# Expert stage of a GNN layer with a mixture of experts: the parts of the chunk sorts and the chunk sizes moved in the plan

## The reference

```python
x = x + gnn(layernorm(x), edges)      # two segment sums over the edges, two 256x256 products, tanh
x = x + ffn(layernorm(x))             # below

rh = relu(f @ router_w1 + router_b1)                       # 256 -> 128
expert_logits = softmax(rh @ router_w2 + router_b2)        # 6 experts
top_w, top_i = top_k(expert_logits, 2)
routing_weights = softmax(top_w)
h1 = relu(f @ expert_w1[e] + expert_b1[e])                 # 256 -> 256, for every expert e
h2 = relu(h1 @ expert_w2[e] + expert_b2[e])
expert_out = h2 @ expert_w3[e] + expert_b3[e]
combined = sum over the two chosen experts of expert_out * routing weight
```

## Time and profile before

| | |
|---|---|
| time, median of 3 runs | 3660.32 us (3653.39 to 3662.05) |
| profiled execution: time, span | 3686.31 us, 3684.6 us |
| TensorE busy in the span | 2478.4 us, 67% |
| VectorE busy | 2074.6 us, 56% |
| ScalarE busy | 942.4 us, 26% |
| POOL busy | 2218.0 us, 60% |
| mean granted TensorE clock | 0.788 |
| last stage, first to last tile's addition | 3173.06 to 3660.97 us |

### The profile page before, as it was taken

The page is one execution under the profiler, slowest core; times in us unless marked ns, Lnnn a source line. Parts: engine busy times, 40 slices in busy tenths (PEclk is TensorE's granted clock), DMA queues, the critical chain, the costliest instruction groups (busy, mean ns, idle before and its releaser), DMA issues.

```text
span 3684.6 us, 37872 instructions
## 1 busy us (share of the span) xinstructions
PE 2478.4 (67%) x8589; PEld 1420.2 (39%) x8589; DVE 2074.6 (56%) x5241; ACT 942.4 (26%) x2586; POOL 2218.0 (60%) x2267
## 2 busy tenths in 40 slices
PE   6463355556655666658677777777777776689786
PEld 4343233334333333436223222222222322678675
DVE  8999444444444444445466656666666666545554
ACT  5686000000000000003222222222222224446342
POOL 5387566666666666666666666666666661225345
PEclk7667577777777677668788888888888887889887
DMA  0200433333333333344533333333333336225344
GB/s 23 71 3 10 140 90 93 93 89 93 90 94 89 92 92 91 92 88 77 158 91 91 91 90 92 92 90 90 92 90 93 92 87 122 88 70 164 92 119 125
DMA packets 169722, 334.22 MB, mean 91 GB/s; under 512 B 39463, under 2 KB 104704, under 8 KB 169508
## 3 DMA queue, kind: packets, MB, share of 16 engines
q0 software_dynamic: 100064, 264.05, 26.6%
q1 hardware_dynamic: 69444, 67.75, 5.6%
HBM read 289.39 MB, written 42.06 MB: 90 GB/s over the span
## 4 chain that ended last, share of the span: by engine, by line
PE 47%; DVE 20%; issue 13%; another core or an unknown queue 12%; DVEq 4%; ACT 3%; DMA 1%; POOL 0%; POOLq 0%; SPq 0%; ACTq 0%
PE ps L934 34%; DVE big L970 10%; PE ps L1693 5%; DVEq L943 3%; PE ps L1673 2%; DVE graph L963 2%; ACT big L574 2%; PE ps L1060 1%; DVE big L753 1%; DVE arena L745 1%; DVEq L970 1%; PE ps L1651 1%; PE ps L989 1%; DVE node L686 0%
## 5 line engine op out<-in xcount | busy, mean ns | idle before, releaser
L934 PE MATMUL ps<-arena,graph 128*128 128x258 f32 (+1 forms) x3588 | 1665.4, 608 | 876.6 <-DVE graph L963 528.4
L970 DVE TENSOR_TENSOR big<-ps,big 128x258 f32 (+1 forms) x1794 | 1003.3, 559 | 956.9 <-remote 420.0
L934 PEld LDWEIGHTS ps<-arena,graph 128*128 128x128 f32 x3588 | 758.8, 234 | 1775.5 <-issue 1674.2
L899 POOL DMA_INDIRECT arena<-xn_table,graph x897 | 849.3, 947 | 472.7 <-issue 202.4
L899 POOL DMA_INDIRECT arena<-h_table,graph x897 | 858.6, 957 | 447.7 <-issue 235.0
L963 DVE TENSOR_SCALAR graph<-iota,graph 128x128 f32<-128x128 f32 x1794 | 545.1, 304 | 310.2 <-issue 215.1
L915 ACT ACTIVATE arena<-arena 128x256 f32<-128x256 f32 x897 | 352.3, 413 | 951.0 <-PE ps L934 561.6
L1312 POOL DMA_INDIRECT arena<-xn_table,node x118 | 125.1, 1060 | 341.3 <-PE ps L1651 164.5
L998 ACT ACTIVATE late<-ps 128x256 f32<-128x256 f32 x49 | 18.8, 383 | 1150.1 <-remote 846.4
L493 POOL DMA_INDIRECT edge_list<-big x112 | 158.9, 1419 | 78.7 <-issue 78.7
L537 PE MATMUL ps<-big,arena 128*128 128x224 f16 x832 | 129.9, 327 | 104.1 <-ACT big L574 97.8
(11 more groups left out here) (252 smaller groups left out, 1823.0 us busy)
## 6 DMA issues: line engine op xcount, KB each, us to landing
y_table<-big SPq DMA_DIRECT2D x118, 128.0 KB
arena<-xn_table,graph POOLq DMA_INDIRECT x897
arena<-h_table,graph POOLq DMA_INDIRECT x897
xn_table<-node SPq DMA_DIRECT2D x7, 896.0 KB, 8.3
h_table<-node SPq DMA_DIRECT2D x7, 896.0 KB, 4.1
node<-in_x SPq DMA_DIRECT2D x1, 6144.0 KB
late<-h_table SPq DMA_DIRECT2D x12, 512.0 KB
big<-in_x SPq DMA_DIRECT2D x12, 512.0 KB, 4.6
```

What stands on the lines that cost most here:

```text
L899: e.indirect_dma_start(out=row, out_offset=None, in_=table, in_offset=bass.IndirectOffsetOnAxis(ap=idx[:, k:k + 1], axis=0)).then_inc(s_ro ...
L934: e.matmul(out_, hot[:, k % HOTS, :], moving, start=True, stop=True).then_inc(s_sum[i], 1)
L970: e.tensor_tensor(block, ps[a % BANKS][:, 0:width], block, ALU.add).then_inc(s_add[i], 1)
```

## The change

Three things change, all in the plan. The chunks become 16, 12, 12 and 9 blocks (16, 16, 12 and 5 before), with 37, 29, 29 and 23 tiles, again 118. TensorE's parts of a sort get names of their own: "sums" and "places" (`pe_sums`, `pe_places`; before, `pe_sort` was called for each step and acted in steps 3, 9 and 11). In the sorts of chunks 1 to 3 they stand one tick behind VectorE's step that feeds them, and VectorE's steps stand one to a tick (steps 1 and 2 share one, and step 12 stands with the last placing), so that a sort lasts 14 ticks instead of 7. The sort of chunk 0, ahead of the tiles, has them in the tick of the step as before. And a chunk's routes no longer begin at a chunk's first tile: they follow behind the routes of the chunk before, beside its sort.

```diff
-        cut = [0, 4, 8, 11, NG]
+        cut = [0, 4, 7, 10, NG]
...
-        SORT_STEPS = 13
+        SORT = ((0,), (1,), (2,), (3, "sums"), (4,), (5,), (6,), (7,), (8,), (9, "places"), (10,), (11, "places"), (12,))
+        SORT_SLOWLY = ((0,), (1, 2), (3,), ("sums",), (4,), (5,), (6,), (7,), (8,), (9,), ("places",), (10,), (11,),
+                       ("places", 12))
...
-            def sort_of(s, t, each):
-                for step in range(SORT_STEPS):
-                    put(t + step // each, "sort", s, step)
-                return t + -(-SORT_STEPS // each)
+            def sort_of(s, t, ticks_of):
+                halves = iter(range(2))
+                for i, steps in enumerate(ticks_of):
+                    for step in steps:
+                        if step == "sums":
+                            put(t + i, "sums", s)
+                        elif step == "places":
+                            put(t + i, "places", s, next(halves))
+                        else:
+                            put(t + i, "sort", s, step)
+                return t + len(ticks_of)
...
-            lead = sort_of(0, t, 1)
+            lead = t = z = sort_of(0, t, SORT)
             for s in range(1, NS):
-                t = z = lead + tile0[s - 1]
                 for i, pair in enumerate(pairs[s]):
                     if (s, i) != (1, 0):
                         t = x1_slowly(pair, t)
-                    z = route_slowly(pair, t)
+                    y = route_slowly(pair, t)
                     t += 2 + len(pair)
-                z = sort_of(s, z, 2)
+                t = y
+                z = sort_of(s, max(y, z), SORT_SLOWLY)
```

More of the change, by code:

```diff
@@ L1643, in pe_last @@
                     pe_route(e, n, step[0])
-                elif stage == "sort":
-                    pe_sort(e, n, step[0])
+                elif stage == "sums":
+                    pe_sums(e, n)
+                elif stage == "places":
+                    pe_places(e, n, step[0])
                 elif stage == "turn":
@@ L1726, in pe_route, with pe_sums, pe_places @@
                 m.then_inc(s_lg, 1)
-        def pe_sort(e, s, step):
+        def pe_sums(e, s):
+            n = len(chunks[s])
+            e.wait_ge(s_som, s + 1)
+            if s:
+                e.wait_ge(s_srt, s)
+            e.matmul(ps[7][:, 0:NE * n], below[:, :], member[:, 0:NE * n], start=True, stop=True)
+            e.matmul(ps[7][:, 256:256 + NE * n], ones[:, :], member[:, 0:NE * n], start=True,
+                     stop=True).then_inc(s_sob, 1)
+        def pe_places(e, s, c):
             n, nt = len(chunks[s]), tiles_in[s]
             th = tile_hot[:, 0:2 * n * nt].rearrange("p (a b j) -> p a b j", a=2, b=n)
[L1731 to L1744, removed]
+            e.wait_ge(s_lhot, 2 * s + c + 1)
+            for i in range(n):
+                m = e.matmul(ps[7][:, 0:2 * nt].rearrange("p (a j) -> p a j", a=2), lane_hot[:, i, :],
+                             th[:, :, i, :], start=(c == 0 and i == 0), stop=(c == 1 and i == n - 1))
+            m.then_inc(s_tokp, 1)
         block = ctx.enter_context(nc.Block())
```

## The result

| | before | after |
|---|---|---|
| time, median (us) | 3656.86 (3652.95 to 3662.05, 4 runs) | 3616.38 (3610.67 to 3621.89, 4 runs) |
| ratio to before | 1 | 0.9885, 95% interval 0.9871 to 0.9899 |
| profiled execution: time, span (us) | 3686.3, 3684.6 | 3621.9, 3620.2 |
| its ticks 1 to 117 (us) | 487.9 | 436.4 |
| behind the last tile (us) | 23.6 | 32.2 |

The change takes 40.5 us away; 39.4 had been forecast, from a median of 3660.3 to 3621 us. The two profiled executions differ by 64.4 us, and not all of that is the change's: tick 0 begins at 3151.59 instead of 3173.06, 21.5 us earlier, behind gathering passes that the change doesn't touch. The rest is 51.5 us less in the ticks (forecast 49.5) and 8.6 more behind them (forecast 10.1), 42.9 net.

The account below looks back on a forecast made before the run. TensorE bounds bare ticks at 2.87 us, VectorE's steps the sorts, POOL's gathers the end. Excess falls from 152.3 to 102.8 us, 49.5 less; the end adds 10.1: 39.4 off 3660.3 gives 3621 us, range 3596 to 3648.

Parts of the forecast that it names:

- Sorts bound by waits for each other: Sorts of chunks 1 to 3: VectorE's steps bound them, TensorE and VectorE waiting in turn; 72.5 of 152.3 us excess.
- Ticks 18 to 35: Sort of chunk 1 beside variations, x1 and routes: 22 us of excess (8 to 33), 12.1 of it VectorE's overhang.
- Ticks 43 to 60: Sort of chunk 2 with chunk 0's blocks brought back beside it: 28 us of excess (17 to 42), 7.5 for those blocks.
- Ticks 66 to 79: Sort of nine blocks with only blocks brought back beside it: about 5 us of excess (2 to 12).
- Ticks 1 to 17, 36 to 42: Stretches without sorts, carrying three groups and one group of side work: 11.1 and 3.7 us of excess.
- Blocks brought back: Excess where blocks return beside tiles, priced by rates from the trace: 31.5 us after the change (10 to 45).
- The end: After the last tile, nine blocks gathered instead of five: 8 x 1.27 = +10.1 us, uncertain by at most 1 us.
- Chunk borders and ScalarE's tables: First gathers of a chunk cost nothing; table load before the exponentials 1.5 us a sort, two further table changes at most 1.35 each.
- Overlap better than costed (3596): Rival 1, crowded stages: light ticks make up for heavy ones, excess only 8 and 17 us, 25 us more gone; chance 13%.
- Waits that only spread (3646): Rival 2: steps, exponentials, variations and stores wait for each other; crowded stages cost half as much again, 25 us; chance 12%.
- Half clock in the crowded stages (3680): Rival 3: TensorE at half rate through 36 crowded ticks, 1.65 us more each, 59 us less 39, slower; chance 6%.
- over 0.95: Sign that the forecast is right: TensorE's granted clock in ticks 18 to 60 lies above this value.

Follow-up runs that it names:

- behind only: Kernel before with its chunk sizes, only TensorE's sums and placings one tick behind VectorE's step: 3273.78 us, 0.9897 (second kind); again 3617.06, 0.9891 (first kind).

## Why the prediction was right, point by point

- *Sorts bound by waits for each other.* Right, and shown in both directions: put into the kernel before, the tick between the engines takes 41.8 us of the sorts' 71.1; taken out of the changed kernel, it gives 27.6 back. In the changed kernel TensorE waits 0.0 us before sums and placings.
- *Ticks 18 to 35.* Forecast 22 (74 us), measured 22.3 (73.9) and, on the second kind of chip, 21.6. Counting VectorE's overhang tick by tick gave the right sum; no run prices its terms one by one.
- *Ticks 43 to 60.* Forecast 28 (80 us), measured 32.1 (83.8) and 26.6 (78.3). One tick of 6.7 us is the longest of the run; under 7, as said. The 7.5 us in it were VectorE's additions for blocks brought back. No run takes them out: without POOL's gathers, but with the additions, the stage is 1.3 us shorter. But this stage is 5.0 us longer than that of ticks 18 to 35 on the second kind (78.27 less 73.24), where the forecast has 7.5 less 1.7 = 5.8 for the difference, so the size of the term fits.
- *Ticks 66 to 79.* Forecast 5; measured 8.0 and 3.7.
- *Ticks 1 to 17, 36 to 42.* Forecast 11.1 and 3.7; measured 10.4 and 3.7 (10.4 and 3.5).
- *Blocks brought back.* This is the step that failed, though the sum hid it. Since its ticks overlap those of the third sort, I compare ticks 61 to 117 as a whole: forecast 5 + 1.5 + 31.5 = 38.0; the first kind took 32.3 and the second 2.9. I had rates from one trace, read them as the price of a block at a given spacing, and expected thinner ones to cost less: 17.9 us less in all (8.9 + 25.7 + 14.8 = 49.4 before, 31.5 after). On the second kind eleven ticks with blocks as dense as any cost 0.6 us over bare ones. What the first kind takes longer in the stage hardly follows the spacing: 41.5 us in the kernel before (487.9 less 446.4), 39.8 in "behind only" (445.9 less 406.1), 35.6 after (436.4 less 400.8). So 5.9 us went for 17.9. The rest of the change was too small in the forecast by about as much: 49.5 less 17.9 is 31.6 us, and the second kind shows 45.6 (446.4 less 400.8). There the kernel before keeps 110.6 us of excess, where the forecast left 102.9 to all but blocks, and the changed one 65.0 for 71.3. Two mistakes of 12 and 14 us cancel in the 51.5 of the first kind: that the stage came out within 2 us is luck.
- *What the surplus of the first kind hangs on* is open. It begins where blocks are brought back: the first stands in tick 41, and from tick 0 to tick 40 the two kinds differ by no more than 0.8 us in each of four pairs of traces (before, after twice, "behind only"). Waits without a releaser on the core come to 92 us over all engines in ticks 42 to 117 of the kernel before and to none in ticks 1 to 41; the second kind has none in either. By the number of blocks brought back beside tiles, 44 before and 40 after, it is 0.94 and 0.89 us a block. So on that kind a price by the block, whatever the spacing, isn't ruled out; the run without gathers that could tell was made on the second kind only.
- *Bounds of that term.* The 45 us given for the worst rate are added wrongly: 16.9 us in 11 ticks makes 29.2 in nineteen, less 2.1, and with 7.8 and 6.2 it is 41. Nothing else was worked out from it.
- *The end.* Forecast +10.1, measured +8.6 and +8.4; 32.2 us follow the last tile, not 33 to 34. The interval between gathers was right (1.26 us). What was missed: POOL's first gather of the last chunk comes 1.4 us sooner, since no gathers of chunk 2 are left before it (the kernel before still issues two behind the last tile). That is more than the 1 us of doubt that the forecast allowed.
- *Chunk borders and ScalarE's tables.* In the ticks no turn of a tile waits for its gather, and VectorE never waits for the exponentials. The 1.5 us a stage for ScalarE's table load can't be told from the rest.
- *Overlap better than costed (3596).* No: it would leave 8 and 17 us of excess in the two crowded stages, and they have 22.3 and 32.1 (21.6 and 26.6 on the second kind), about what overhang counted without winning back gives.
- *Waits that only spread (3646).* No: it would put 25 us more into the crowded stages, and TensorE waits for nothing at the hand-overs. Undoing the tick between the engines shows what such waits cost: 0.9972.
- *Half clock in the crowded stages (3680).* Refuted: 0.95 and 0.90 on the first kind, 0.98 and 0.96 on the second, at busy shares of 82 to 88%. The sign "over 0.95" held on the second kind; on the first, where the result was taken, it was just not met in the first stage and missed by 0.05 in the second.
- The rule of the Trainium skill, "TensorE: Matmul & The Clock Gate", section "HAM oscillation — how this bites in real kernels", describes the kernel before rather than the changed one: 0.77 in the old sorts went to 0.95 when their waits were filled, and many short waits did not bring whole stages near the half rate (0.90 to 0.98).

What failed to show in the time: the new sizes, the starts without a pause and the slow spreading. Beside "behind only" on the second kind of chip they take 5.3 us off the stage and put 7.9 on the end; the times, 3273.8 and 3275.6, don't differ. They make the kernel no faster than a nine-tick sort in the old plan.

## What to carry to other kernels

Where two engines hand work to each other in a loop that a third bound sets, put one whole iteration between the producer's step and the consumer's: here that alone was 1.0 to 1.1% of the kernel, and it needed only a sort two ticks longer and routes that begin three ticks sooner. Count what is left as the overhang of the heaviest side work tick by tick, without saving up slack. An excess for which a trace gives only a rate and no instruction has no known cause yet: take out what is suspected, and measure on a second chip, before work is moved for it.

## What the runs showed of the hardware

Chips of two kinds differ by 10% in the same kernel. The kernel before takes 3654 to 3657 us on the one (the result, chips 12 and 15) and 3310 to 3311 on the other (chips 1 and 2). One stretch of 1200 us of the gathering passes, first and second kind (columns as above):

```profile
1800.00:3000.00 1200.00, 908.36 (x1658) 338.36 (x1659) 734.00 (x1645) 326.20 (x835) 786.78 (x823) 0.85 0.31 91
```

```profile
1500.00:2700.00 1200.00, 1012.47 (x2080) 336.14 (x2081) 820.89 (x1873) 395.33 (x977) 902.78 (x982) 0.96 0.38 108
```

In each pass POOL issues 897 gathers, most of them 1.26 us apart on either kind. On the first, some 90 intervals of a pass are over 2 us, one in ten gathers, on the second none or one. In the last stage, from the first blocks brought back on, stalls show on ScalarE, VectorE and POOL with no releaser on the core that the profile could name, as in this row of the kernel before:

```profile
3469.60 0.42 DVE L1358 TENSOR_TENSOR big<-ps,node 128x256 f32<-128x256 f32 x1 [6.81 <-remote]
```

Their cause stays open; no kernel here removed them. The kinds differ by 345 us in the time of the kernel before, of which 42 lie in the ticks of the last stage. What is shown is that the ratio of this change doesn't hang on them: 0.9885 and 0.9900 on the one kind, 0.9892 on the other.
